# Two attention/feed-forward stacks on one core: order of the norm sums, of the scores' maximum and of gelu, and a variance in which GpSimd has one product

## What is computed

```python
x = x + attn_a(layernorm(x))   # 16 heads of 8, "polymax" in place of softmax, causal
x = x + ffn(layernorm(x))      # the stack, below
x = x + attn_b(layernorm(x))   # 16 heads of 8, softmax, causal
x = x + ffn(layernorm(x))      # the same stack with the same weights
```

```python
x = attn_layer(shift_tokens(x), Wqkv, q_scale, k_scale, Wo) + x
x = ffn_layer(shift_tokens(x), ln_g, ln_b, W1, b1, W2, b2) + x
# attn_layer: q, k = l2norm(.) * scale, rotary position; windows of 32 tokens that look one
#   window back; softmax(q k^T * 8 + mask) v, 16 heads of 64; times Wo
# ffn_layer: xn = (x - mean) / sqrt(var + 1e-5) * g + b;  a, gate = split(xn @ W1 + b1)
#   (a * gelu(gate)) @ W2 + b2     with 341 hidden columns for each half
# shift_tokens: the second half of the channels comes from the token before
```

## Time and profile before

| | |
|---|---|
| time, median of 3 runs (lowest to highest) | 4276.1 us (4270.4 to 4289.2) |
| the profiled execution: its own time, its span | 4277.9 us, 4276.2 us |
| PE busy | 3789.2 us, 89% |
| DVE busy | 3357.8 us, 79% |
| ACT busy | 2526.5 us, 59% |
| POOL busy | 2501.7 us, 59% |
| granted clock of TensorE, mean of the span | 0.971 of 2.4 GHz |

### The profile page before, as it was taken

The page is one execution under the profiler, slowest core; times in us unless marked ns, Lnnn a source line. Parts: engine busy times, 40 slices in busy tenths (PEclk is TensorE's granted clock), DMA queues, the critical chain, the costliest instruction groups (busy, mean ns, idle before and its releaser), DMA issues. The chain is left out here.

```text
span 4276.2 us, 153902 instructions
## 1 busy us (share of the span) xinstructions
PE 3789.2 (89%) x67640; PEld 2277.3 (53%) x67640; DVE 3357.8 (79%) x4385; ACT 2526.5 (59%) x3236; POOL 2501.7 (59%) x2036
## 2 busy tenths in 40 slices
PE   6887799999999999999678886899999999999996
PEld 3232456666666666666333333566666666666664
DVE  7998788888888888888354436788888888888884
ACT  5886456666666666666223453566566665666664
POOL 0001677777787777876100005787777877777772
PEclk8999999999999999999789998999999999999998
DMA  0001232323323223222000002323323233232221
GB/s 20 1 1 42 67 87 67 91 72 79 89 67 91 73 78 90 64 70 62 17 1 1 1 1 78 90 74 85 78 73 89 73 84 80 74 88 71 69 63 40
DMA packets 165604, 260.98 MB, mean 61 GB/s; under 512 B 58574, under 2 KB 79818, under 8 KB 164938
## 3 DMA queue, kind: packets, MB, share of 16 engines
q1 hardware_dynamic: 164936, 251.13, 22.5%
HBM read 48.61 MB, written 1.05 MB: 12 GB/s over the span
## 5 line engine op out<-in xcount | busy, mean ns | idle before, releaser
L1382 POOL TENSOR_TENSOR f_k_rotated<-f_rope_ak,f_rope_bk 128x1024 f32<-128x1024 f32 x192 | 454.1, 2365 | 271.6 <-DVE f_rope_bk L1432 271.6
L1098 PE MATMUL banks<-f_wqkv,H 128*128 128x512 f32 x1152 | 561.7, 611 | 23.2 <-DVE f_rope_bk L1432 12.2
L1098 PE MATMUL banks<-f_wqkv,G 128*128 128x512 f32 x1152 | 552.9, 602 | 1.0 <-issue 1.0
L1364 POOL MEMSET f_kT<- 128x256 f32 x2 | 0.6, 312 | 840.5 <-POOLq L514 461.1
L1382 POOL TENSOR_TENSOR f_q_rotated<-f_rope_aq,f_rope_bq 128x1024 f32<-128x1024 f32 x192 | 454.9, 2369 | 52.9 <-DVE f_rope_bq L1432 52.6
L1155 PEld LDWEIGHTS banks<-f_O_T,f_wo 128*128 128x128 f32 x3072 | 372.5, 192 | 106.0 <-issue 93.2
L1322 ACT ACTIVATE f_V<-banks 128x1024 f32<-128x1024 f32 x192 | 196.0, 1021 | 377.6 <-PE banks L1098 377.6
L1155 PE MATMUL banks<-f_O_T,f_wo 128*128 128x128 f32 x3072 | 375.4, 275 | 11.0 <-issue 8.4
L1429 DVE TENSOR_TENSOR f_rope_aq<-banks,f_rope 128x1024 f32<-128x1024 f32 x192 | 235.0, 1224 | 184.7 <-ACT f_sqq L1287 169.2
L1394 POOL TENSOR_TENSOR f_q_rotated<-f_q_rotated,f_inverse_norm 128x1024 f32<-128x1024 f32 x192 | 365.5, 1903 | 15.0
L1376 POOL TENSOR_TENSOR f_E<-f_E,f_row_inverse 128x1024 f32<-128x1024 f32 x192 | 367.9, 1916 | 8.0 <-DVE f_row_inverse L1464 8.0
(11 more groups left out here) (207 smaller groups left out, 9075.0 us busy)
## 6 DMA issues: line engine op xcount, KB each, us to landing
f_P_T_paired<-f_P_T SPq DMA_DIRECT2D x1536, 64.0 KB, 2.0
f_V_previous<-f_V SPq DMA_DIRECT2D x192, 384.0 KB, 3.9
f_V_previous<-f_V SPq DMA_DIRECT2D x192, 128.0 KB, 2.5
f_wqkv<-in_L_ffn_Wqkv SPq DMA_DIRECT2D x48, 384.0 KB, 3.7
f_rope<-in_rope SPq DMA_DIRECT2D x24, 512.0 KB, 4.2
f_wo<-in_L_ffn_Wo SPq DMA_DIRECT2D x12, 512.0 KB, 5.5
f_w<-in_L_ffn_W SPq DMA_DIRECT2D x12, 341.0 KB
f_w<-in_L_ffn_W SPq DMA_DIRECT2D x24, 64.0 KB
```

The costliest lines, as they stand in the source:

```text
L1098: mm = nc.tensor.matmul(ps[:, o * BLK:(o + 1) * BLK], xs, w[:, c * INNER + o * BLK:c * INNER + (o + 1) * BLK], start=True, stop=True)
L1382: nc.gpsimd.tensor_tensor(qk[i][:], ra[i][:], rb[i][:], ALU.add).then_inc(radd.sem, 1)
```

## The change

Four things change.

1. On VectorE the sum of K's squares and the clamp stand directly behind K's rotary products, ahead of the maximum and the subtraction.
2. On ScalarE the seeds of the norms (Ln, Exp) stand behind the copy of V (and behind gelu, where there is one), ahead of the copy of O and the Exp of the scores.
3. Gelu stands behind the copy of V instead of ahead of it; its table load is written out and stays ahead of the copy.
4. The inverse root of the variance: VectorE writes -0.5 (var + eps) into `var`; ScalarE takes Ln with scale -2, Exp, and then squares the seed; GpSimd multiplies the squared seed by `var` (one product in place of four operations); VectorE multiplies the centred block by the gain and the seed, and in a second operation by (var + 1.5).

```diff
@@ ScalarE, in each slot
                 if live(s):
                     squares(n, 1, k_mm, PK)
-                if (b := feed(s, 11)) is not None:
-                    act.wait_ge(f_gev.sem, f_gev.at(blk(b)))
-                    nc.scalar.activation(ge[:].rearrange("p j t -> p (j t)"), ge[:].rearrange("p j t -> p (j t)"),
-                                         ACT.Gelu).then_inc(f_ge.sem, 1)
+                if feed(s, 11) is not None:
+                    nc.scalar.preload_act_table_set("gelu_and_others")
                 if live(s):
                     act.wait_ge(v_mm.sem, v_mm.at(n))
...
                     nc.scalar.activation(V[n % 4][:], PV_F, ACT.Copy).then_inc(v_ev.sem, 1)
-                if feed(s, 11) is not None:
+                if (b := feed(s, 11)) is not None:
+                    act.wait_ge(f_gev.sem, f_gev.at(blk(b)))
+                    nc.scalar.activation(ge[:].rearrange("p j t -> p (j t)"), ge[:].rearrange("p j t -> p (j t)"),
+                                         ACT.Gelu).then_inc(f_ge.sem, 1)
                     nc.scalar.preload_act_table_set("natural_log_exp_and_others")
+                if live(s):
+                    act.wait_ge(clamped.sem, clamped.at(n))
+                    act.wait_ge(newton.sem, newton.past(n - 1))
+                    nc.scalar.activation(lg[:], ss[n % 2][:], ACT.Ln).then_inc(seeded.sem, 1)
+                    act.wait_ge(seeded.sem, seeded.at(n, 1))
+                    nc.scalar.activation(y0[:], lg[:], ACT.Exp, scale=-0.5).then_inc(seeded.sem, 1)
                 if live(s - 3):
...
                 if live(s - 1):
                     act.wait_ge(sbd.sem, sbd.at(n - 1))
                     nc.scalar.activation(E[(n - 1) % 2][:], E[(n - 1) % 2][:], ACT.Exp).then_inc(expd.sem, 1)
-                if live(s):
-                    act.wait_ge(clamped.sem, clamped.at(n))
-                    act.wait_ge(newton.sem, newton.past(n - 1))
-                    nc.scalar.activation(lg[:], ss[n % 2][:], ACT.Ln).then_inc(seeded.sem, 1)
-                    act.wait_ge(seeded.sem, seeded.at(n, 1))
-                    nc.scalar.activation(y0[:], lg[:], ACT.Exp, scale=-0.5).then_inc(seeded.sem, 1)
                 if (b := feed(s, 8)) is not None:
                     act.wait_ge(f_eps.sem, f_eps.at(blk(b)))
                     act.wait_ge(f_nt.sem, f_nt.past(blk(b) - 1))
-                    nc.scalar.activation(xsq[:], var[:], ACT.Ln).then_inc(f_seed.sem, 1)
+                    nc.scalar.activation(xsq[:], var[:], ACT.Ln, scale=-2.0).then_inc(f_seed.sem, 1)
                     act.wait_ge(f_seed.sem, f_seed.at(blk(b), 1))
+                    act.wait_ge(f_xn.sem, f_xn.past(blk(b) - 1))
                     nc.scalar.activation(vy0[:], xsq[:], ACT.Exp, scale=-0.5).then_inc(f_seed.sem, 1)
+                    act.wait_ge(f_seed.sem, f_seed.at(blk(b), 2))
+                    nc.scalar.activation(xsq[:], vy0[:], ACT.Square).then_inc(f_seed.sem, 1)
@@ GpSimd
                 if (b := feed(s, 8)) is not None:
                     pool.wait_ge(f_seed.sem, f_seed.at(blk(b)))
-                    nc.gpsimd.tensor_tensor(xsq[:], vy0[:], vy0[:], ALU.mult).then_inc(f_nt.sem, 1)
-                    nc.gpsimd.tensor_tensor(xsq[:], xsq[:], var[:], ALU.mult).then_inc(f_nt.sem, 1)
-                    nc.gpsimd.tensor_scalar(xsq[:], xsq[:], -0.5, 1.5, ALU.mult, ALU.add).then_inc(f_nt.sem, 1)
-                    nc.gpsimd.tensor_tensor(var[:], xsq[:], vy0[:], ALU.mult).then_inc(f_nt.sem, 1)
+                    pool.wait_ge(f_xn.sem, f_xn.past(blk(b) - 1))
+                    nc.gpsimd.tensor_tensor(var[:], xsq[:], var[:], ALU.mult).then_inc(f_nt.sem, 1)
@@ VectorE
                 if live(s):
                     rotate(s, 1, k_mm, PK)
+                    sums(n, 1)
+                    dve.wait_ge(red.sem, red.at(n))
+                    nc.vector.tensor_scalar(ss[n % 2][:], ss[n % 2][:], 1e-24, None, ALU.max).then_inc(clamped.sem, 1)
                 if live(s - 1):
...
-                if live(s):
-                    sums(n, 1)
-                    dve.wait_ge(red.sem, red.at(n))
-                    nc.vector.tensor_scalar(ss[n % 2][:], ss[n % 2][:], 1e-24, None, ALU.max).then_inc(clamped.sem, 1)
...
                 if (b := feed(s, 8)) is not None:
                     dve.wait_ge(f_var.sem, f_var.at(blk(b)))
-                    dve.wait_ge(f_nt.sem, f_nt.past(blk(b) - 1))
-                    nc.vector.tensor_scalar(var[:], bank(5), EPS, None, ALU.add).then_inc(f_eps.sem, 1)
+                    dve.wait_ge(f_xn.sem, f_xn.past(blk(b) - 1))
+                    nc.vector.tensor_scalar(var[:], bank(5), EPS, -0.5, ALU.add, ALU.mult).then_inc(f_eps.sem, 1)
                 if (b := feed(s, 9)) is not None:
...
-                    nc.vector.scalar_tensor_tensor(xn[:], xcs[:], vec[b // NBLK % 2][:, 0:1], var[:], ALU.mult, ALU.mult)\
+                    nc.vector.scalar_tensor_tensor(xn[:], xcs[:], vec[b // NBLK % 2][:, 0:1], vy0[:], ALU.mult, ALU.mult)\
                         .then_inc(f_xn.sem, 1)
+                    dve.wait_ge(f_xn.sem, f_xn.at(blk(b), 1))
+                    nc.vector.scalar_tensor_tensor(xn[:], var[:], 1.5, xn[:], ALU.add, ALU.mult).then_inc(f_xn.sem, 1)
```

More of the change, by code:

```diff
@@ L931, in ffn_stack @@
         f_xc, f_sq, f_xcs, f_var, f_eps, f_seed = sig("x_centered"), sig("x_squared"), sig("x_centered_copied"), \
-            sig("var_done"), sig("eps_added"), sig("var_seeded", 2)
-        f_nt, f_xn, f_xb = sig("var_newton_steps", 4), sig("xn_scaled"), sig("xn_ready")
+            sig("var_done"), sig("eps_added"), sig("var_seeded", 3)
+        f_nt, f_xn, f_xb = sig("var_newton_steps"), sig("xn_scaled", 2), sig("xn_ready")
         f_g, f_gev, f_ge, f_a, f_hm = sig("gate_done", 3), sig("gate_evacuated", 3), sig("gelu_done"), \
@@ L1398, in _ @@
                     pool.wait_ge(f_seed.sem, f_seed.at(blk(b)))
-                    nc.gpsimd.tensor_tensor(xsq[:], vy0[:], vy0[:], ALU.mult).then_inc(f_nt.sem, 1)
-                    pool.wait_ge(f_nt.sem, f_nt.at(blk(b), 1))
-                    nc.gpsimd.tensor_tensor(xsq[:], xsq[:], var[:], ALU.mult).then_inc(f_nt.sem, 1)
-                    pool.wait_ge(f_nt.sem, f_nt.at(blk(b), 2))
-                    nc.gpsimd.tensor_scalar(xsq[:], xsq[:], -0.5, 1.5, ALU.mult, ALU.add).then_inc(f_nt.sem, 1)
-                    pool.wait_ge(f_nt.sem, f_nt.at(blk(b), 3))
-                    nc.gpsimd.tensor_tensor(var[:], xsq[:], vy0[:], ALU.mult).then_inc(f_nt.sem, 1)
+                    pool.wait_ge(f_xn.sem, f_xn.past(blk(b) - 1))
+                    nc.gpsimd.tensor_tensor(var[:], xsq[:], var[:], ALU.mult).then_inc(f_nt.sem, 1)
                 if (b := feed(s, 9)) is not None:
```

## The result

The changed kernel takes 4483.2 us (median of 4 runs, 4480.8 to 4485.6) against 4279.1 us before: a ratio of 1.048, with a 95% interval of 1.0465 to 1.049. The forecast was 4495 us, the range 4390 to 4540.

The account below looks back on a forecast made before the run. TensorE was taken to wait for K's normalisation, with the subtraction's chain 0.68 us behind. 4278 us plus 208 (4.73 us a period, 44 times) plus 9 for the early slots gave 4495 us, range 4390 to 4540.

Parts of the forecast that it names:

- The second chain and its slack: Output projection must wait for the subtraction: slack 0.68 us, new start k + 10.43 in slot 3 (k: K's projection starts).
- The clamp in GpSimd's addition: VectorE's clamp is held until GpSimd's addition of K ends, to R + 4.90 (R: K's rotation starts on VectorE).
- Slots 0 and 2: Slots by s % 4, K's projection to the next: 17.41 us for 0 to 2, 16.55 us for 3.
- Seeds, gelu and the copy of O: ScalarE's new order costs nothing behind the late subtraction; with gelu in slot 3 K's normalisation is barely in time.
- The Square: ScalarE's added Square of the seed makes K's rotation 0.89 us late in the slot following slot 0; bounds zero and 0.9.
- The scalings' stall: In slot 1 VectorE's two scalings of xn wait for GpSimd's normalisations, making Q's rotation 1.72 us late; bounds 0 and 1.72.
- The first slots of each call: Eight slots ahead of each call's first feed get only the later subtraction: some 0.6 us each, 9 us in all.
- The sum: Period of four slots: 69.67 us, with the stalled scaling 71.39, against 66.66; 4.73 us more, 44 times: 208 us.

Follow-up runs that it names:

- split variance: Changed kernel without ScalarE's Square: GpSimd squares the seed, multiplies, adds 1.5 and does the second scaling, VectorE scales xn once; 4424.9 us, ratio 1.0349.
- run 23: Not a run's label: the words read "Over the run", the changed kernel's (4483.2 us), then "23 of the 192 output projections", a count.
- sum and clamp back: Changed kernel with the sum of K's squares and the clamp behind the subtraction again, all else as changed; 4272.6 us, ratio 0.9992.
- order alone: Kernel before the change with only the sum of K's squares and the clamp moved ahead of maximum and subtraction; 4533.8 us, ratio 1.0604.
- variance back: Changed kernel with the variance as before: four operations on GpSimd, no Square, one scaling on VectorE; 4494.7 us, ratio 1.0516.

## Why the prediction was right, point by point

- **The second chain and its slack.** Right. The step was to look not at what TensorE waits for but at what is next: 0.68 us of slack in the subtraction. The output projection starts at k + 10.43 in slot 3 (1196.03 - 1185.60), the very number of the sum; the 0.06 us from the subtraction to TensorE, an estimate in the prediction, are 0.05 here (1195.98 to 1196.03).
- **The clamp in GpSimd's addition.** Right in mechanism and size: end at R + 4.92 (R + 4.90 in the sum), 1.32 us as the median, all 192 of them. The runs with no clamp, with a reduction in its place and with the clamp on GpSimd show it from three sides.
- **Slots 0 and 2.** 17.5 us against 17.41, and slot 3 16.66 against 16.55. The term that was too small is the output projection's: from its start to the next product it is 1.89 us behind an idle TensorE (1196.03 to 1197.92), and 1.78 where it follows other work. TensorE's wait ahead of it, put at some 1.8 us in nearly every slot, has medians of 1.4, 1.8 and 1.5 us in slots 0, 1 and 3.
- **Seeds, gelu and the copy of O.** Right: they cost nothing while the subtraction is late. The spare time that I gave gelu in slot 3 (barely in time) was enough.
- **The Square.** 0.89 us, as forecast.
- **The scalings' stall.** Right that VectorE is held in this form too, and right that the first slips in or the second waits; the term was too large. 1.72 us was put down, and 1.1 us a period measured. The step that was off: K's normalisation loses 0.45 us to the first scaling and not the scaling's whole length, and the second scaling ends sooner behind it, so the add of the block's output starts at R + 11.45 and not at R + 11.92. Where VectorE has no second scaling (the split variance) it starts at R + 10.28, close to the R + 10.20 of the sum. What is left makes the transposes of Q late, whose bank waits for the residual add, and k with them; I had it reach R by way of Q's rotation. The two don't add up: from k to R it is 3.11 us in slot 2 (median), against 3.08.
- **The first slots of each call.** Wrong: 0.6 us each was put down, 9 us in all, and 23 us measured (10.5 and 12.6 us for the eight slots of the two calls). The step that failed: nothing was put down for TensorE's clock. The first four slots of a call differ little. The next four take 18.1 to 19.5 us against 15.87, as TensorE is idle for 2.6 to 3.6 us ahead of the output projection, and this one then takes 3.5 to 3.8 us. Timeline of PE in the same slot, before and after:

```profile
494.13 2.02 PE L1155 MATMUL banks<-f_O_T,f_wo 128*128 128x128 f32 x16 [1.16 <-DVE f_E L1476]
...
496.21 3.75 PE L1155 MATMUL banks<-f_O_T,f_wo 128*128 128x128 f32 x16 [3.02 <-DVE f_E L1478]
```

The start is k + 10.45, as in the sum (10.43; k is 485.76 here), so the whole excess lies behind it. From 496.2 to 500.0 the granted clock is 0.50, its lower level of 1.2 GHz. Over the run 23 of the 192 output projections take more than 2.5 us; before, none does.

- **The sum.** 71.39 us a period was forecast and 71.38 is the mean measured. That is luck, as the terms aren't so close: the stall was 0.6 us too large, the output projection 0.1 us too small in most slots, and the mean period is 0.23 us above the sum of the four medians. The period before, 66.66 us by two rows, is 66.93 over 42 periods. This makes 4.45 us a period and not 4.73. The whole is closer than its terms, too: the 42 periods between slots 8 and 92 lost 187 us, the first eight slots of the two calls 23 us (forecast 9), and what follows slot 92 became some 3 us shorter; together 207.6 us between the two spans, where 217 (208 + 9) was forecast.

The expectations of the experiments were wrong more often, five of ten times outside their ranges. Three times (sum and clamp back, order alone, variance back) I carried a stall over from one order to another without asking anew which of the two engines comes first there, and in the last of these I left out TensorE's clock as well. Without the clamp I took too small a stall of the scalings, and with the split variance I left out the slots that are longer than the median.

## What to carry to other kernels

Before moving an instruction ahead in a queue, look at what the other engines do at the new place, not only at what it delays: here a short fp32 tensor_scalar on SBUF on VectorE (0.18 us alone) took as long as GpSimd's running tensor_tensor had still to go, 0.9 to 2.1 us, and everything behind it on VectorE paid. When a wait on the critical path is to be removed, measure the slack of the next wait first; here it was 0.68 us, against the sum's 1.24 us alone. Small work whose result GpSimd's next step needs can be put on GpSimd itself: the clamp takes 0.28 us there, and the kernel went from 4483 to 4252 us.

## What the runs showed of the hardware beyond this

- An instruction that VectorE holds ready gets in between two GpSimd instructions issued back to back: the clamp of 0.96 us in the run with the order alone, and the first scaling (0.87 us) in the changed kernel. It waits for the one that is running and not for those queued.
- Both engines can be the one that is held. GpSimd's normalisation goes from 1.90 to 2.36 us when a scaling of 0.71 us was issued 0.11 us ahead of it, and the scaling goes from 0.70 to 2.27 us when it is issued inside a normalisation.
- TensorE's granted clock fell to its lower level (1.2 GHz) behind an idle time of 2.66 us in a steady period, and the 16 products of the output projection took 3.62 us, not 1.95. The idle time alone doesn't settle it: behind a median of 2.44 us 33 of 42 output projections were slow (variance back, slot 1), behind a median of 1.81 us still 12 of 42 (changed kernel).
